# A two-layer windowed transformer on one NeuronCore: the second tile's values, queries and transposes moved, and the exponential's table loaded earlier

## The chip, the cores and the metric

The kernel runs on one core of one Trainium2 chip. The core has five engines, each with its own instruction queue, worked off in order: PE (TensorE, matrix products and transposes), ACT (ScalarE, functions and copies), DVE (VectorE), POOL (GpSimd) and SP (SyncE, which only issues transfers here). PE writes to PSUM, 128 partitions by eight banks of 512 float32 columns; ACT and DVE read PSUM, POOL doesn't. The metric is the time of one execution in microseconds (us).

## The reference

Eight batches of 256 tokens with 256 channels. First a gated cross-attention, then two layers of a local-attention transformer with a gated GELU, all in float32:

```python
x = x + tanh(g_xattn) * xattn(layernorm(x), ctx, ctx, mask)       # one head of 256
y = layernorm(x)
for l in range(2):
    h = shift_token(y)                       # half of the channels come from the token before
    q, k, v = split(h @ wqkv[l], 3)          # 8 heads of 64
    q, k = rotary(l2norm(q) * q_scale, l2norm(k) * k_scale)
    o = local_attention(q, k, v)             # window of 128: a token sees its own and the previous window
    y = y + o @ wo[l]
    h = layernorm(shift_token(y)) * ln_g + ln_b
    a, g = split(h @ w1[l] + b1[l], 2)       # 682 hidden channels
    y = y + (a * gelu(g)) @ w2[l] + b2[l]
x = x + tanh(g_ffn) * y
```

## The kernel before

A first stage does the cross-attention of the eight batches. Then come 17 steps. Step s does the attention half of one batch in one layer (batch s, layer 0 for s below 8, then layer 1) together with the feed-forward half of the batch of step s-1; step 0 has only an attention half, step 16 only a feed-forward half. Steps 2 to 7 and 9 to 14 are two loops on the engines ("loop steps" below); 0, 1, 8, 15 and 16 are written out. Every engine's order within a step is written by hand; semaphores join the engines. The 256 tokens are two tiles, t = 0 and 1, of 128 rows. Float32 products are made of three products of rounded high and low parts (`split_product`, L422).

On PE a step runs: `project` (queries, keys and values of both tiles, j = 0, 1, 2; tile 0 uses banks 0, 1, 2, tile 1 banks 3, 4 and, for its values, bank 2 again), then `up(0)` to `up(5)`, the first feed-forward product in six chunks in banks 5 and 6 by turns, with the transposes of queries and keys (`tr_heads(t, j)`, L580) in between. Then `scores_own(0)` (L592) and `scores_both(0)` (L598) for the first two heads, five pieces `down(0)` to `down(4)` of the second feed-forward product, and a loop over heads h of `scores`, `tr_probs(h)` (transposes of the probabilities, L607 to L609), more `down`, and `weighted` (L621). Last come the transposes of the next batch and the output projection.

The other engines, per head h: DVE's `row_min(h)` (L1153) masks the scores and takes each row's minimum, ACT's `exps(h)` (L855) takes the exponentials, DVE's `row_sum(h)` (L1159) the reciprocals of their sums, POOL's `normalise(h)` (L1357) multiplies, PE transposes, ACT's `probs_T(h)` (L861) copies.

In the feed-forward half, for each chunk c: ACT's `gelu(c)` (L825, the sixth L828), DVE's `gated(c)` (L1134), ACT's `high_u(c)` (L834, chunks 0 to 4), POOL's `low_u(c)` (L1339), PE's `down(c)`. The last chunk has 42 rows, and its high part is cast by DVE (`high_last_u`, L1142), which waits until ACT has done `high_u(4)`. PE's `down(4)` waits for `low_u(4)`, which needs `high_u(4)` too. Before `low_u(4)` POOL does an addition (L1381).

ACT also copies values (`values(t)`, L818), transposed queries (`queries_T(t)`, L840) and keys (`keys_T(t)`, L846) out of PSUM. Its function tables hold one set at a time; a Gelu after an Exp, and the other way round, needs an `ACT_TABLE_LOAD`. The Gelu's is brought forward by a dummy activation of one column, `table_touch` (L895); the Exp's stands right ahead of `exps(0)`.

Of the kernel before, what the change touches and what calls it, by code (L numbers as in the profile page):

```python
# [18 lines left out]
P = 128  # L19
# [4 lines left out]
ACT = mybir.ActivationFunctionType  # L24
# [5 lines left out]
HEADS, DH = 8, 64  # L30
# [19 lines left out]
def build(nc, x, ctx_in, mask, g_xattn, g_ffn, Wq, bq, Wk, bk, Wv, bv, ln_gamma, ln_beta,  # L50
          wqkv, q_scale, k_scale, wo, ln_g, ln_b, w1, b1, w2, b2, rot_tab, win_mask, ident_in, shift_in, out):
    NB, S, D = x.shape
    T = S // P
# [22 lines left out]
    with st:  # L76
# [3 lines left out]
        def sem(name):  # L80
            return st.enter_context(nc.semaphore(name))
# [83 lines left out]
        def bank(i):  # L165
            return ps[:, i, :]
# [7 lines left out]
        w_high, w_ready, w2_ready = sem("w_high"), sem("w_ready"), sem("w2_ready")  # L174
        b1_mm, b1_done, w1_scaled = sem("b1_mm"), sem("b1_done"), sem("w1_scaled")
        zeros_set, nhalf_set, tanh_done, prep_done = sem("zeros_set"), sem("nhalf_set"), sem("tanh_done"), sem("prep_done")
        touch_set = sem("touch_set")
        dve_passed, pool_passed = sem("dve_passed"), sem("pool_passed")

        x_loaded, c_loaded, m_loaded, xres_loaded = (  # L180
# [227 lines left out]
        def _(pe):  # L408
# [113 lines left out]
            def step(s, la, lf):  # L522
                f = s - 1

                def project(t, parts):

                    i = 0 if t == 0 else 3
                    if t == 0 and 0 in parts:
                        pe.wait_ge(yT_done, s + 1)
                        if isinstance(s, int) and s == 0:  # L530
                            pe.wait_ge(xnT_done, NB)
                            pe.wait_ge(kT_x, KC * NB)
                            pe.wait_ge(qT_x, KC * NB)
                            pe.wait_ge(v_x, NB)
                    elif 0 in parts:
                        wait(pe, pT_done, HEADS * s)
                    for j in parts:
                        if j == 2:
                            if t == 0:
                                wait(pe, x1_done, s)  # L540
                            else:
                                pe.wait_ge(v_done, T * s + t)
                        if t == 0 and isinstance(s, int) and s in (0, NB):
                            pe.wait_ge(w_ready, VPIECES * la + j + 1)
                        o = bank(i + j) if j < 2 else bank(2)
                        for k in range(KC):
                            c0 = k * YTC - k + t * P
                            last = split_product(o, lambda a: yT[a][:, c0:c0 + P],
                                                 lambda a: wqkv_hl[a][:, k, j * INNER:(j + 1) * INNER],
                                                 k == 0, k == KC - 1)  # L550
                        last.then_inc((qk_mm, qk_mm, v_mm2)[j], 1)

                def up(c):

                    i = 5 + c % 2
                    if c == 0:
                        pe.wait_ge(hT_done, s)
                        if lf == 1 or (isinstance(s, int) and s == 1):
                            pe.wait_ge(w_ready, VPIECES * (lf + 1))
                            pe.wait_ge(w2_ready, 2 * (lf + 1))  # L560
                    if c < 2:
                        pe.wait_ge(o_done, PAIRS * s)
                    else:
                        pe.wait_ge(u_raw, HC * f + c - 1)
                    for o, r, n in up_parts(c):
                        for k in range(KC):
                            last = split_product(ps[0:r, i, n * S:(n + 1) * S],
                                                 lambda a: w1_hl[a][:, k, o:o + r], lambda a: hT[a][:, k, :],
                                                 k == 0, k == KC - 1)
                    last.then_inc(up_mm, 1)  # L570

                def tr_heads(t, j):

                    i = 0 if t == 0 else 3
                    if j == 0:
                        pe.wait_ge(sq_done, 2 * (T * s + t + 1))
                    if j == 0:
                        pe.wait_ge(ks_done, T * s + t + 1)
                    for c in range(PAIRS):
                        last = nc.tensor.transpose(bank(i + j)[:, c * P:(c + 1) * P],  # L580
                                                   t1[:, t, j * INNER + c * P:j * INNER + (c + 1) * P],
                                                   ident[:])
                    last.then_inc(qk_tr, 1)
# [44 lines left out]
                def down(n):  # L628

                    t, c = n // HC, n % HC  # L630
                    if t == 0:
                        pe.wait_ge(u_done, HC * f + c + 1)
                    last = split_product(bank(7)[:, t * D:(t + 1) * D], lambda a: u[a][:, c, t * P:(t + 1) * P],
                                         lambda a: w2_hl[a][:, c, :], c == 0, c == HC - 1)
                    if n == T * HC - 1:
                        last.then_inc(dn_mm, 1)
# [39 lines left out]
                if A:  # L676
                    tr_heads(0, 1)
                if F:
                    for c in range(3, HC):
                        up(c)  # L680
                if A:
                    tr_heads(1, 0)
                    tr_heads(1, 1)
                if A:
                    pe.wait_ge(q_done, T * s + 1)
                    pe.wait_ge(k_done, T * s + 1)
                    pe.wait_ge(v_done, T * (s + 1))
                    scores_own(0)
                    pe.wait_ge(q_done, T * (s + 1))
                    pe.wait_ge(k_done, T * (s + 1))  # L690
                    scores_both(0)
                n = 0
                if A and F:
                    for n in range(HC - 1):
                        down(n)
                    n = HC - 1
                if A:
                    for h in range(HEADS + 1):
                        if h in (0, 1, 3):
                            scores_own((h + 3) // 2)  # L700
                            scores_both((h + 3) // 2)
                        if h < HEADS:
                            tr_probs(h)
                        if isinstance(s, int) and s in (0, NB) and h == HEADS - 1:
                            bias_products(la)
                        if F:
                            while (n - HC + 1) * HEADS < (T * HC - 2 - HC + 1) * h:
                                down(n)
                                n += 1
                        if h and h % 2 == 0:  # L710
                            weighted(h // 2 - 1)
                    if not (isinstance(s, int) and s == STEPS - 1):
                        pe.wait_ge(ynext_in, 16 * (s + 2))
                        pe.wait_ge(mn_done, T * HEADS * (s + 1))
                        transpose_rows(y_next, 0).then_inc(y_tr, 1)
# [20 lines left out]
        def _(act):  # L736
# [68 lines left out]
            def step(s, la, lf):  # L805
# [9 lines left out]
                def values(t):  # L815
                    act.wait_ge(v_mm2, T * s + t + 1)
                    wait(act, pv_mm, HEADS * s)
                    A(vs[:, t, :], bank(2), ACT.Copy).then_inc(v_done, 1)  # L818

                def gelu(c):  # L820
                    act.wait_ge(up_mm, HC * f + c + 1)
# [9 lines left out]
                def high_u(c):  # L831
                    act.wait_ge(u_raw, HC * f + c + 1)
                    r = hrows[c]
                    A(u[0][0:r, c, :], u_full[c % 4][0:r, :], ACT.Copy).then_inc(u_high, 1)  # L834

                def queries_T(t):
                    i = 0 if t == 0 else 3
                    act.wait_ge(qk_tr, 2 * (T * s + t) + 1)
                    wait(act, s_mm2, HEADS * s)
                    A(qT[:, :, t * P:(t + 1) * P], bank(i).rearrange("p (c n) -> p c n", c=PAIRS),  # L840
                      ACT.Copy).then_inc(q_done, 1)

                def keys_T(t):
                    i = 0 if t == 0 else 3
# [55 lines left out]
                    gelu(1)  # L900
                    high_u(0)
                if la is not None:
                    queries_T(0)
                if lf is not None:
                    gelu(2)
                if la is not None:
# [1 line left out]
                if lf is not None:  # L908
                    high_u(1)
                    gelu(3)  # L910
                    high_u(2)
                    gelu(4)
                    high_u(3)
                    gelu(5)
                if la is not None:
                    queries_T(1)
                    keys_T(1)
                if lf is not None:
                    high_u(4)
                if la is not None:  # L920
# [18 lines left out]
        def _(dve):  # L939
# [131 lines left out]
            def step(s, la, lf):  # L1071
# [95 lines left out]
                def row_statistics():  # L1167
# [6 lines left out]
                    for t in range(T):  # L1174
                        wait_apart(dve, dve_passed, (hbn_a, 2 * (T * f + t + 1)))
                        V.bn_aggr(hmv[:, t, :], hst[:, t, :, :]).then_inc(hbn, 1)  # L1176

                start = isinstance(s, int) and s == 0
                if isinstance(s, int) and s == NB:
                    low_parts(1, True)  # L1180
# [35 lines left out]
                    add_context(NB - 1)  # L1216
                if F:
                    gated(4)
                    gated(5)
                    high_last_u()  # L1220
                if start:
# [223 lines left out]
```

## Time and profile before

| what | value |
|---|---|
| median of three runs | 821.9 us (819.35 to 823.16) |
| the profiled execution's own time | 824.24 us |
| its span, first to last instruction | 822.4 us |
| busy: PE, DVE, ACT, POOL | 730.5, 527.0, 486.9, 437.2 us |
| mean granted clock of PE | 0.964 |

The span leaves 1.8 us of the profiled execution's time outside it. Busy time says how long an engine had an instruction under way, not what held the others up; that is read from the waits and from the chain of work that ended last. A loop step takes 40.8 us (its first square on ACT starts at 327.36 in step 5 and at 368.15 in step 6).

### The profile page before, as it was taken

Reading aid. Unit: us, or ns where it says so; the run is one execution under the profiler, and the core shown is the slowest. Engines: PE = TensorE matmul, PEld = TensorE weight load, DVE = VectorE, ACT = ScalarE, POOL = GpSimd, SP = SyncE. Lnnn points to the kernel's source line nnn. Section 1 sums busy time; section 2 is a strip of 40 time slices with the busy share of each in tenths; the row PEclk is TensorE's granted clock in tenths of the full one; section 3 lists DMA queues with packets and bytes.
Section 4 is the critical chain, followed back from the end, with each engine's and each line's share of the span. In section 5 each row is a group of like instructions: output and inputs, shape, how many; then the busy total and the mean of one; then the engine's idle time right before and its main releaser. Section 6 shows DMA issues by size and latency. Waiting matters only on the chain.

```text
span 822.4 us, 17078 instructions
## 1 busy us (share of the span) xinstructions
PE 730.5 (89%) x4984; PEld 608.3 (74%) x4984; DVE 527.0 (64%) x1470; ACT 486.9 (59%) x1289; POOL 437.2 (53%) x592
## 2 busy tenths in 40 slices
PE   5898766989999999999998998999999999999967
PEld 4787654877878787878786877877777777777746
DVE  2898896384848484847475836657575766666732
ACT  2443425366767575757577665757575757575742
POOL 0433464473838383838383646738383737373712
PEclk9999987799999999999999998999999999999988
DMA  6444423160000000000101001010101010101000
GB/s 209 144 149 140 125 47 108 48 232 16 24 17 23 21 18 24 14 32 6 37 2 38 1 2 51 2 52 0 51 0 51 0 51 0 51 0 39 1 27 13
DMA packets 32786, 38.36 MB, mean 47 GB/s; under 512 B 8476, under 2 KB 22896, under 8 KB 32752
## 3 DMA queue, kind: packets, MB, share of 16 engines
q1 hardware_dynamic: 32752, 37.95, 14.4%
q8 instruction: 16, 0.26, 0.1%
q14 instruction: 18, 0.15, 0.1%
HBM read 29.55 MB, written 8.39 MB: 46 GB/s over the span
## 4 chain that ended last, share of the span: by engine, by line
PE 56%; DVE 13%; ACT 11%; issue 10%; POOL 5%; DMA 3%; SPq 1%; DVEq 1%; ACTq 0%; POOLq 0%
PE ps L422 39%; ACT pr L855 4%; PE ps L621 4%; PE ps L598 3%; DMA arena<-x 2%; PE ps L517 2%; DVE arena L955 2%; PE ps L580 2%; PE ps L592 1%; PE ps L415 1%; POOL xrs L1275 1%; ACT pT L861 1%; PE ps L625 1%; DVE sm L1153 1%; POOL pr L1357 1%
## 5 line engine op out<-in xcount | busy, mean ns | idle before, releaser
L1357 POOL TENSOR_SCALAR pr<-pr,rl 128x128 f32<-128x128 f32 (+1 forms) x256 | 107.6, 433 | 80.5 <-DVE rl L1159 80.4
L855 ACT ACTIVATE pr<-sm,mn 128x128 f32<-128x128 f32 (+1 forms) x256 | 113.4, 445 | 20.6 <-DVE mn L1153 20.1
L1153 DVE CUSTOM_DVE_ANT_0 sm<-ps,wmask 128x128 f32<-128x128 f32 (+1 forms) x256 | 79.9, 354 | 44.4 <-PE ps L598 38.5
L422 PE MATMUL ps<-hT_hi,w_hi 128*128 128x256 f32 (+1 forms) x352 | 103.4, 294 | 1.7 <-DVE hT_lo L1125 1.4
L422 PE MATMUL ps<-hT_hi,w_lo 128*128 128x256 f32 (+1 forms) x352 | 101.0, 287 | 0.0
L422 PE MATMUL ps<-hT_lo,w_hi 128*128 128x256 f32 (+1 forms) x352 | 100.2, 285 | 0.0
L1328 POOL TENSOR_TENSOR rn<-ss,nhalf 128x16 f32<-128x16 f32 x32 | 96.7, 3023 | 2.7
L813 ACT ACTIVATE sqb<-ps 128x512 f32<-128x512 f32 x64 | 38.0, 596 | 95.5 <-PE ps L422 88.6
L422 PE MATMUL ps<-wqkv_hi,yT_hi 128*128 128x512 f32 x192 | 80.3, 418 | 12.5 <-DVE arena L997 5.2
L1273 POOL TENSOR_SCALAR hrs<-hmv 128x2 f32<-128x2 f32 x16 | 3.1, 193 | 150.6 <-DVE hmv L1176 150.6
L1339 POOL TENSOR_TENSOR u_lo<-u_pair,u_hi 128x256 fp32r<-128x256 f32 x64 | 68.9, 1085 | 23.8 <-ACT u_hi L834 21.7
L422 PE MATMUL ps<-wqkv_lo,yT_hi 128*128 128x512 f32 x192 | 77.1, 402 | 0.0
L422 PE MATMUL ps<-wqkv_hi,yT_lo 128*128 128x512 f32 x192 | 77.0, 401 | 0.0
L825 ACT ACTIVATE gl<-ps,b_sb 128x256 f32<-128x256 f32 x80 | 38.0, 475 | 58.6 <-PE ps L422 58.6
L422 PEld LDWEIGHTS ps<-hT_hi,w_hi 128*128 128x128 f32 (+1 forms) x352 | 67.6, 192 | 4.7 <-DVE hT_lo L1125 2.5
L422 PEld LDWEIGHTS ps<-hT_lo,w_hi 128*128 128x128 f32 (+1 forms) x352 | 67.9, 193 | 0.1
L422 PEld LDWEIGHTS ps<-hT_hi,w_lo 128*128 128x128 f32 (+1 forms) x352 | 67.2, 191 | 0.0
L861 ACT ACTIVATE pT<-ps 128x384 f32<-128x384 f32 x128 | 61.2, 480 | 7.9 <-PE ps L609 6.9
L422 PE MATMUL ps<-w_hi,u_hi 128*128 128x256 f32 x192 | 64.0, 333 | 1.4 <-POOL u_lo L1339 1.3
L607 PE MATMUL ps<-ident,pr 128*128 128x128 f32 x128 | 41.6, 325 | 20.1 <-POOL pr L1357 17.9
L1146 DVE TENSOR_TENSOR oT_lo<-ps,oT_hi 128x256 fp32r<-128x256 f32 x64 | 27.1, 423 | 49.7 <-ACT oT_hi L866 48.1
L607 PEld LDWEIGHTS ps<-ident,pr 128*128 128x128 f32 x128 | 17.9, 140 | 51.8 <-POOL pr L1357 48.9
(148 smaller groups left out, 2129.8 us busy)
## 6 DMA issues: line engine op xcount, KB each, us to landing
arena<-x SPq DMA_DIRECT2D x16, 256.0 KB, 3.5
ystream<-arena SPq DMA_DIRECT2D x16, 256.0 KB, 2.0
y_next<-ystream SPq DMA_DIRECT2D x16, 256.0 KB, 2.8
y_res<-ystream SPq DMA_DIRECT2D x16, 256.0 KB, 2.6
arena<-L_ffn_w SPq DMA_DIRECT2D x6, 640.0 KB
arena<-ctx SPq DMA_DIRECT2D x8, 256.0 KB, 3.9
arena<-mask_BxSxS_ik SPq DMA_DIRECT2D x8, 256.0 KB, 2.8
xmid<-arena SPq DMA_DIRECT2D x8, 256.0 KB, 2.0
```

The costliest lines, as they stand in the source:

```text
L422: last = mm(out, lhsT(a), rhs(b), start=(start and i == 0), stop=(stop and i == 2))
L607: nc.tensor.transpose(b[:, 0:P], p[:, 2 * P:3 * P], ident[:])
L621: mm(b[j * DH:(j + 1) * DH, 0:S], vs[:, 0, h * DH:(h + 1) * DH], pT[:, h % 4, P:3 * P], start=True, stop=False)
L813: A(sqb[:, j * INNER:(j + 1) * INNER], bank(i + j), ACT.Square).then_inc(sq_done, 1)
L825: A(gl[:, c % 2, :], ps[:, 5 + c % 2, S:2 * S], ACT.Gelu, bias=b1_sb[:, lf, 1, c:c + 1]).then_inc(gl_done, 1)
L855: A(pr[:, h % NS, a:b], sm[:, h % NS, a:b], ACT.Exp, bias=mn[:, h, t:t + 1], scale=-1.0, accum_out=ls[:, h, t:t + 1]).then_inc(e_done, 1)
L861: A(pT[:, h % 4, :], bank(3 + h % 2)[:, 0:3 * P], ACT.Copy).then_inc(pT_done, 1)
L1146: V.tensor_tensor(oT[1][:, pair, :], bank(5 + pair % 2)[:, 0:S], oT[0][:, pair, :].bitcast(F32), ALU.subtract).then_inc(o_done, 1)
L1153: V.tensor_tensor_reduce(sm[:, h % NS, a:b], bank(h % SB)[:, a:b], wmask[:, a:b], 1.0, -NEG, ALU.add, ALU.min, mn[:, h, t:t + 1]).then_inc ...
L1328: G.tensor_tensor(rn[:, t, :], ss[:, t, :], nhalf[:], ALU.pow).then_inc(rn_done, 1)
L1339: G.tensor_tensor(u[1][0:r, c, :], u_full[c % 4][0:r, :], u[0][0:r, c, :].bitcast(F32), ALU.subtract).then_inc(u_done, 1)
L1357: G.tensor_scalar(pr[:, h % NS, a:b], pr[:, h % NS, a:b], rl[:, h, t:t + 1], 1.0, ALU.mult, ALU.mult).then_inc(pn_done, 1)
```

## The change

Four things move within a step. Tile 1's values go to bank 6 instead of bank 2, so their product no longer waits for ACT to empty bank 2; it waits for bank 6's last user in the step before, and `up(1)`, which writes bank 6 next, waits for both copies of values. Tile 1's transposed queries are copied by DVE, between `gated(4)` and `gated(5)`, with a semaphore of their own (`q1_done`), instead of by ACT. Tile 1's transposes stand ahead of `up(5)` instead of behind it, and ACT's `keys_T(1)` ahead of `high_u(3)`. And ACT does a dummy exponential of one column right behind `gelu(5)`, ahead of `high_u(4)`. The order of the `down` pieces is written another way and stays what it was.

```diff
@@ PE: project
                             else:
-                                pe.wait_ge(v_done, T * s + t)
+                                wait(pe, o_done, PAIRS * s)
...
-                        o = bank(i + j) if j < 2 else bank(2)
+                        o = bank(i + j) if j < 2 else bank(2 + 4 * t)
@@ PE: up(c)
                     if c < 2:
                         pe.wait_ge(o_done, PAIRS * s)
+                        if c == 1 and la is not None:
+                            pe.wait_ge(v_done, T * (s + 1))
@@ PE: step
                 if F:
-                    for c in range(3, HC):
+                    for c in range(3, HC - 1):
                         up(c)
                 if A:
                     tr_heads(1, 0)
                     tr_heads(1, 1)
+                if F:
+                    up(HC - 1)
...
                     scores_own(0)
-                    pe.wait_ge(q_done, T * (s + 1))
+                    pe.wait_ge(q1_done, s + 1)
                     pe.wait_ge(k_done, T * (s + 1))
                     scores_both(0)
@@ ACT: values(t)
-                    A(vs[:, t, :], bank(2), ACT.Copy).then_inc(v_done, 1)
+                    A(vs[:, t, :], bank(2 + 4 * t), ACT.Copy).then_inc(v_done, 1)
@@ ACT: step
                     gelu(4)
+                if la is not None:
+                    keys_T(1)
+                if lf is not None:
                     high_u(3)
                     gelu(5)
                 if la is not None:
-                    queries_T(1)
-                    keys_T(1)
+                    A(table_touch[:, 1:2], table_touch[:, 0:1], ACT.Exp)
                 if lf is not None:
                     high_u(4)
@@ DVE
+                def queries_T():
+                    dve.wait_ge(qk_tr, 2 * (T * s + 1) + 1)
+                    wait(dve, s_mm2, HEADS * s)
+                    V.tensor_copy(qT[:, :, P:S], bank(3).rearrange("p (c n) -> p c n", c=PAIRS)).then_inc(q1_done, 1)
...
                 if start:
                     context(NB - 1)
                     gate_context(NB - 1)
                     add_context(NB - 1)
                 if F:
                     gated(4)
+                if A:
+                    queries_T()
+                if F:
                     gated(5)
                     high_last_u()
```

ACT's queue in a loop step, from `gelu(4)` to the first exponential, before (`gl` is a gelu's result, `u_hi` a high part, `qT` and `kT` the copied queries and keys, `pr` the exponentials):

```order
L825 ACTIVATE gl<-ps,b_sb 128x256 [waits u_raw,up_mm]
L834 ACTIVATE u_hi<-hn 128x256 [waits u_raw]
L821 REGISTER_ALU
L828 ACTIVATE gl<-ps,b_sb 42x256 [waits u_raw,up_mm]
L840 ACTIVATE qT<-ps 128x4x128 [waits s_mm2,qk_tr]
L846 ACTIVATE kT<-ps 128x4x128 [waits qk_tr]
L834 ACTIVATE u_hi<-u_pair 128x256 [waits u_raw]
L850 ISA
L855 ACT_TABLE_LOAD [waits rl_done]
L855 ACTIVATE pr,ls<-sm,mn 128x128 [waits mn_done]
```

and the same stretch of the changed kernel:

```order
L830 ACTIVATE gl<-ps,b_sb 128x256 [waits u_raw,up_mm]
L849 ACTIVATE kT<-ps 128x4x128 [waits qk_tr]
L839 ACTIVATE u_hi<-hn 128x256 [waits u_raw]
L826 REGISTER_ALU
L833 ACTIVATE gl<-ps,b_sb 42x256 [waits u_raw,up_mm]
L922 ACT_TABLE_LOAD
L922 ACTIVATE table_touch<-table_touch 128x1
L839 ACTIVATE u_hi<-u_pair 128x256 [waits u_raw]
L853 ISA
L858 ACTIVATE pr,ls<-sm,mn 128x128 [waits rl_done,mn_done]
```

The keys moved up, the queries are gone, and the table load with its dummy now stands ahead of the fifth high part instead of behind it.

DVE's queue in the written-out step 0 of the changed kernel, from the last additions of the first stage (`arena`, `xst`, `xmv`) to the first `row_min` (`sm`, `mn`):

```order
L987 TENSOR_TENSOR arena<-arena 128x512 [waits xmid_stored,xrb_done,tg_done]
L952 BN_STATS xst<-arena 128x6 [waits xmid_done]
L952 BN_STATS xst<-arena 128x6
L955 BN_AGGR xmv<-xst 128x2 [waits stats_mid] x2
L1186 COPY qT<-ps 128x4x128 [waits qk_tr]
L1158 ISA sm,mn<-ps,wmask 128x128 [waits cst2_in,s_mm2]
L1158 ISA mn 128x1
L1158 ISA sm,mn<-ps,wmask 128x256
```

Here the copy of queries stands behind what is left of the first stage, right ahead of the first `row_min`; before, the rows around it were the same without it, and ACT made that copy.

## Rows read from the trace of the kernel before

**Rows 1.** Chain of work that ended last, step 5: start us, us, what

```profile
345.73 0.60 ACT kT L846
...
347.17 1.98 PE ps L422 x15
```

**Rows 2.** Timeline of PE, step 5: start us, us, instruction, idle before

```profile
334.26 0.50 PE L422 MATMUL ps<-wqkv_hi,yT_hi 128*128 128x512 f32 x1 [0.33 <-ACT vs L818]
...
335.76 0.28 PE L422 MATMUL ps<-hT_hi,w_hi 128*128 128x256 f32 x1
...
343.74 0.28 PE L422 MATMUL ps<-hT_hi,w_hi 128*106 128x256 f32 x1
...
344.45 1.04 PE L580 MATMUL ps<-ident,turned 128*128 128x128 f32 x8
...
346.47 0.70 PE L598 MATMUL ps<-kT,qT 64*128 64x256 f32 x4 [0.56 <-ACT kT L846]
...
350.57 0.33 PE L607 MATMUL ps<-ident,pr 128*128 128x128 f32 x1 [0.56 <-POOL pr L1357]
...
352.04 0.33 PE L607 MATMUL ps<-ident,pr 128*128 128x128 f32 x1
...
353.18 0.33 PE L607 MATMUL ps<-ident,pr 128*128 128x128 f32 x1 [0.24 <-POOL pr L1357]
```

**Rows 3.** Timeline of ACT, step 5

```profile
336.01 0.20 ACT L895 ACTIVATE table_touch<-table_touch 128x1 f32<-128x1 f32 x1
...
344.74 0.47 ACT L828 ACTIVATE gl<-ps,b_sb 42x256 f32<-42x256 f32 x1
...
346.35 0.42 ACT L834 ACTIVATE u_hi<-u_pair 128x256 fp32r<-128x256 f32 x1
346.78 1.28 ACT L855 ACT_TABLE_LOAD   x1
348.11 0.40 ACT L855 ACTIVATE pr<-sm,mn 128x128 f32<-128x128 f32 x1
```

**Rows 4.** Timeline of DVE, step 5

```profile
334.82 0.68 DVE L1125 TENSOR_TENSOR hT_lo<-ps,hT_hi 128x512 fp32r<-128x512 f32 x1
...
346.80 0.29 DVE L1142 CAST u_hi<-u_pair 42x256 fp32r<-42x256 f32 x1 [1.08 <-ACT u_hi L834]
347.43 0.29 DVE L1153 CUSTOM_DVE_ANT_0 sm<-ps,wmask 128x128 f32<-128x128 f32 x1 [0.34 <-PE ps L598]
```

**Rows 5.** Timeline of POOL, step 5

```profile
345.48 1.26 POOL L1381 TENSOR_TENSOR arena<-x,b_bc 128x512 f32<-128x512 f32 x1
346.84 1.52 POOL L1339 TENSOR_TENSOR u_lo<-u_pair,u_hi 128x256 fp32r<-128x256 f32 x2
...
351.15 0.84 POOL L1357 TENSOR_SCALAR pr<-pr,rl 128x128 f32<-128x128 f32 x2 [0.63 <-DVE rl L1159]
```

**Rows 6.** Timeline of POOL and DVE in step 1, which is written out

```profile
183.78 0.73 POOL L1339 TENSOR_TENSOR u_lo<-u_pair,u_hi 128x256 fp32r<-128x256 f32 x1 [0.51 <-ACT u_hi L834]
183.81 0.85 DVE L1142 CAST u_hi<-u_pair 42x256 fp32r<-42x256 f32 x1 [1.14 <-ACT u_hi L834]
184.58 0.28 DVE L1153 CUSTOM_DVE_ANT_0 sm<-ps,wmask 128x128 f32<-128x128 f32 x1
```

**Rows 7.** Timeline of DVE and PE in step 0

```profile
131.83 0.29 DVE L1153 CUSTOM_DVE_ANT_0 sm<-ps,wmask 128x128 f32<-128x128 f32 x1
...
133.12 1.06 PE L598 MATMUL ps<-kT,qT 64*128 64x256 f32 x4
...
134.36 0.29 DVE L1153 CUSTOM_DVE_ANT_0 sm<-ps,wmask 128x128 f32<-128x128 f32 x1 [0.67 <-PE ps L598]
```

**Rows 8.** Chain of work that ended last, end of step 0

```profile
140.48 5.80 DMA arena<-L_ffn_w
146.33 7.45 PE ps L517 x44
```

**Rows 9.** Two stretches: length; busy PE, PEld, DVE, ACT, POOL; PE's clock; DMA

```profile
508.00:512.00 4.00, 2.18 (x10) 1.43 (x8) 3.92 (x8) 2.16 (x6) 2.94 (x6) 1.00 0.00 0
512.00:516.00 4.00, 3.63 (x14) 2.90 (x15) 3.55 (x6) 3.54 (x7) 3.92 (x3) 0.72 0.02 4
```

More of the change, by code:

```diff
@@ L176, in build @@
         zeros_set, nhalf_set, tanh_done, prep_done = sem("zeros_set"), sem("nhalf_set"), sem("tanh_done"), sem("prep_done")
-        touch_set = sem("touch_set")
+        touch_set, q1_done = sem("touch_set"), sem("q1_done")
         dve_passed, pool_passed = sem("dve_passed"), sem("pool_passed")
@@ L683, in step, with downs @@
                     tr_heads(1, 1)
+                if F:
+                    up(HC - 1)
+                n = 0
+                def downs(upto):
+                    nonlocal n
+                    while F and n < upto:
+                        down(n)
+                        n += 1
                 if A:
-                    pe.wait_ge(q_done, T * s + 1)
+                    pe.wait_ge(q_done, s + 1)
                     pe.wait_ge(k_done, T * s + 1)
@@ L688, in step @@
                     scores_own(0)
-                    pe.wait_ge(q_done, T * (s + 1))
+                    pe.wait_ge(q1_done, s + 1)
                     pe.wait_ge(k_done, T * (s + 1))
                     scores_both(0)
[L692 to L697, printed above, removed]
+                    downs(5)
                     for h in range(HEADS + 1):
@@ L705, in step @@
                             bias_products(la)
[L706 to L709, printed above, removed]
+                        downs(5 + min(5, (5 * h + 7) // 8))
                         if h and h % 2 == 0:
@@ L834, in high_u @@
                     A(u[0][0:r, c, :], u_full[c % 4][0:r, :], ACT.Copy).then_inc(u_high, 1)
-                def queries_T(t):
-                    i = 0 if t == 0 else 3
-                    act.wait_ge(qk_tr, 2 * (T * s + t) + 1)
+                def queries_T():
+                    act.wait_ge(qk_tr, 2 * T * s + 1)
                     wait(act, s_mm2, HEADS * s)
-                    A(qT[:, :, t * P:(t + 1) * P], bank(i).rearrange("p (c n) -> p c n", c=PAIRS),
-                      ACT.Copy).then_inc(q_done, 1)
+                    A(qT[:, :, 0:P], bank(0).rearrange("p (c n) -> p c n", c=PAIRS), ACT.Copy).then_inc(q_done, 1)
                 def keys_T(t):
@@ L902, in step @@
                 if la is not None:
-                    queries_T(0)
+                    queries_T()
                 if lf is not None:
@@ L1176, in row_statistics, with queries_T @@
                         V.bn_aggr(hmv[:, t, :], hst[:, t, :, :]).then_inc(hbn, 1)
+                def queries_T():
+                    dve.wait_ge(qk_tr, 2 * (T * s + 1) + 1)
+                    wait(dve, s_mm2, HEADS * s)
+                    V.tensor_copy(qT[:, :, P:S], bank(3).rearrange("p (c n) -> p c n", c=PAIRS)).then_inc(q1_done, 1)
                 start = isinstance(s, int) and s == 0
@@ L1218, in step @@
                     gated(4)
+                if A:
+                    queries_T()
+                if F:
                     gated(5)
```

## The prediction

> **What bounds the kernel now.** I read the chain of work that ended last first, then the timelines of PE, ACT, DVE and POOL over one loop step, step 5, and then the written-out steps 0 and 1. The other eleven loop steps repeat step 5 to a few hundredths of a microsecond. In the chain the reader is to see that PE carries most of a step, and that it is handed to other engines where PE waits: ACT's copy of keys, then scores and five `down` pieces [rows 1]. PE's own timeline shows four waits in step 5 that the change touches: 0.33 us for ACT's copy of values, 0.56 for ACT's copy of keys ahead of `scores_both(0)`, 0.56 for POOL ahead of `tr_probs(0)`, 0.24 ahead of `tr_probs(2)` [rows 2]. From `tr_probs(2)` on the chain runs without slack to the step's end. So what counts is when `tr_probs(2)` starts.
>
> **Values in a bank of their own.** `project(1, 2)` no longer waits, but `up(0)`, right behind it, needs DVE's low part, which ends at 334.82 + 0.68 = 335.50 [rows 4]. PE follows a release by about 0.14 (keys end at 346.33, `scores_both(0)` starts at 346.47 [rows 1, 2]), so `up(0)` starts at 335.64 instead of 335.76: 0.12 gained, not 0.33. The new wait of `up(1)` for both values costs nothing: ACT copies the second right behind its `table_touch` at 336.01 [rows 3], 0.6 us long like the keys, and `up(1)` comes twelve products behind `up(0)`.
>
> **Transposes ahead of `up(5)`.** They start where `up(5)` did, at 343.74 - 0.12 = 343.62, and end 1.04 later, 344.66; `up(5)` is pushed back by about 0.87 (the record of 1.04 less a drain that overlaps, my estimate) and its result is there at about 345.4 [rows 2].
>
> **ACT.** `keys_T(1)` 344.69 to 345.29 (0.60 [rows 1]), `high_u(3)` to 345.6, `gelu(5)` 345.62 to 346.09, which is 0.88 later than now. Then the table load, 1.28, the touch, 0.20 of which the next instruction overlaps some 0.1, and only then `high_u(4)`: 347.51 to 347.92 instead of 346.35 to 346.77, 1.15 later [rows 3]. The load itself is no new cost, since one stands in each step now; at present it lies beside `row_min(0)`, and ends at 348.06, just when `exps(0)` can start at 348.11. The cover that it loses is that: `high_u(4)` used to be ahead of it, and three engines wait for `high_u(4)`.
>
> **Who waits for it.** DVE's cast of the last chunk waits for it by semaphore, and `row_min(0)` is queued behind the cast: cast 347.95, `row_min(0)` at about 348.27 instead of 347.43, and `exps(0)`, 0.68 behind it as now, at 348.95 instead of 348.11, 0.84 later [rows 3, 4]. POOL's addition is done by then (its `low_u(3)` moves with `high_u(3)`, so it ends at about 347.6), and `low_u(4)` runs 347.99 to 348.72, 1.15 later than now [rows 5]. PE's `scores_both(0)` has its queries from DVE (344.8 to 345.4, priced as the 0.68 of DVE's other 512-column instruction from PSUM [rows 4]) and starts at 345.6 instead of 346.47. That gain of 0.87 is given back at once: four `down` pieces of 0.4 each later PE stands at `down(4)`, about 347.8, until `low_u(4)` at 348.76; the five pieces end at 349.25, against 347.17 + 1.98 = 349.15 now [rows 1]. So `scores(1)` is 0.1 later, and everything that hangs on `exps(0)` is 0.84 later: its reciprocal, POOL's multiplication and `tr_probs(0)`, which goes from 350.57 to 351.41 [rows 2].
>
> **What slack takes up.** Behind `tr_probs(0)` PE's queue holds scores, `tr_probs(1)`, a `down`, `tr_probs(2)`. The last waited 0.24, and `tr_probs(1)` at 352.04 came 0.05 behind POOL's 351.15 + 0.84 [rows 2, 5], so some slack lies there as well. I put both at 0.35 and have 0.5 us left per loop step (between 0.3, if the slack is 0.5, and 0.7). Twelve loop steps: 6.0 us.
>
> **Written-out steps 1, 8, 15.** There the cast already takes 0.85 and `row_min(0)` starts right behind it, without waiting for PE [rows 6]. So all of `high_u(4)`'s 1.15 reaches `exps(0)`, less 0.35: 0.8 each, 2.4 us (0.5 to 1.1 each; step 1 may be the low end, since DVE holds its `up(5)` back).
>
> **Step 0.** No feed-forward half, no cast, and the table is already Exp's. But the copy of queries, which ACT did early, now stands on DVE behind the rest of the first stage, where `row_min(0)` started at 131.83. Copy 0.68, answer of PE 0.14, and from the start of such a pair of scores to its `row_min` 134.36 - 133.12 = 1.24 [rows 7]: 2.06 later, 2.0 in the sum. The step's chain runs on over a store, the feed-forward weights' load and the products that wait for them at 146.33 [rows 8], and that load is issued behind DVE work which follows `row_min(2)`; nothing hides it. Bounds: 0.7, the copy alone, if PE's part were hidden, to 2.1. Step 16 is unchanged.
>
> **Sum.** 6.0 + 2.4 + 2.0 = 10.4 us on the profiled execution's 824.24, so 834.6. That execution lies 2.3 over the median of 821.9; for a median I say 832. With the bounds (12 x 0.3 to 0.7, 3 x 0.5 to 1.1, 0.7 to 2.1) 5.8 to 13.8, hence 828 to 836 for this case.
>
> **Rivals.**
> - *The cast is blocked in the loop steps too.* In step 1 POOL's `low_u(4)` started 0.03 ahead of the cast, and the cast took 0.85, until POOL's 0.73 had passed; in step 5 the cast came first by 0.04 and took 0.29 [rows 4 to 6]. In step 5 POOL was then busy with its addition until 346.74; in the changed kernel it will be waiting for `high_u(4)` as in step 1. Then `row_min(0)` comes 0.77 behind the cast's start, not 0.32: 0.45 to 0.55 more in twelve steps, 6 us, 838. Against it: in the loop steps DVE woke 0.03 after ACT's end, POOL takes 0.07. I go by the short cast. The Trainium skill (SBUF — State Buffer, "Who interferes with whom") calls the port pair that DVE's copies and POOL share an exclusive lock that goes to whoever issues first; by that rule it hangs on those 0.04 us, and the sum would be the one or the other.
> - *The delay is taken up.* If PE's slack behind `tr_probs(0)` is as large as 0.84, only the 0.1 of `scores(1)` counts in a loop step: 1.2 + 1 + 2.0, about 826. For it: `exps(2)` hangs on `scores(1)`, not on `exps(0)`. Against it: PE shows only 0.24 of wait there.
> - *Faster.* If `high_u(4)` came no later than now, the wait of 0.56 ahead of `scores_both(0)` and the 0.12 would be won in 15 steps, 10 us, with step 0's loss 814. It decides at `high_u(4)` ending by 346.8 in step 5's time. Against it stands the load's 1.28 in ACT's queue, ahead of it, and `gelu(5)` behind the transposes.
> - *PE's clock falls.* PE would stand 1.0 us at `down(4)` and 1.2 at `tr_probs(0)`. Around step 9's start PE was busy 2.18 of 4 us, and the granted clock then averaged 0.72 over 4 us, part of it at the lower of the two levels, 1.2 GHz [rows 9]. Some 1.2 us per step, 12 steps: 846. Against it: that stall was one piece.
> - *It does nothing:* the order shows every piece moved, so I give this none of its own.
>
> **How the numbers follow.** Forecast 0.62, blocked cast 0.13, taken up 0.13, faster 0.05, clock 0.07. About 0.5%, 4.1 us, is what a measurement of this kernel can tell from no change: faster below 817.8, slower above 826.0. Faster is the third rival, 0.05; same is the second, 0.13, and 0.01 of others; the rest, 0.81, is slower. The range from 825 to 840 takes in the forecast, the blocked cast and half of the second rival, 0.8 in all.
>
> **What would show it.** In the changed trace: `scores_both(0)` without a wait for keys, 0.8 us earlier behind `up(4)`; a wait of about 1 us ahead of `down(4)` on POOL's `low_u(4)`; the table load right behind `gelu(5)`; DVE's wait ahead of the cast grown from 1.08 to over 1.5 and the cast's length (0.29 or 0.85); `tr_probs(0)`'s wait on POOL over 1 us; the loop step's length, 41.3 against 40.8; in step 0 `row_min(0)` about 2 us later. A `high_u(4)` less than 0.5 us late, or PE not waiting ahead of `tr_probs(0)`, would make the prediction wrong.

## The result, and the profile after

The changed kernel takes 832.41 us (median), the kernel before 821.69 on the same chip: 1.0141 times as long, 95% interval 1.0108 to 1.0175. Forecast were 832 us and a range of 825 to 840. The profiled execution took 832.07 us; its span is 830.3 us, 7.9 more than before, and PE is as busy as before (730.6 us).

Step 5 starts 0.93 us later than before (its first square stands at 328.29 instead of 327.36). Whoever takes 0.93 off the rows below can lay them beside [rows 2 to 5]. A step now lasts 41.17 us, before 40.79. First PE's timeline, step 5 of the changed kernel:

```profile
334.61 0.48 PE L422 MATMUL ps<-wqkv_hi,yT_hi 128*128 128x512 f32 x1
...
336.49 0.38 PE L422 MATMUL ps<-hT_hi,w_hi 128*128 128x256 f32 x1 [0.23 <-DVE hT_lo L1130]
...
344.57 1.03 PE L582 MATMUL ps<-ident,turned 128*128 128x128 f32 x8
...
346.57 0.60 PE L600 MATMUL ps<-kT,qT 64*128 64x256 f32 x4
...
349.82 0.38 PE L422 MATMUL ps<-w_hi,u_hi 128*128 128x256 f32 x1 [1.03 <-POOL u_lo L1352]
...
350.16 0.28 PE L422 MATMUL ps<-w_hi,u_lo 128*128 128x256 f32 x1
350.37 0.49 PE L594 MATMUL ps<-kT,qT 64*128 64x128 f32 x4
...
352.38 0.33 PE L609 MATMUL ps<-ident,pr 128*128 128x128 f32 x1 [1.08 <-POOL pr L1370]
...
354.47 0.33 PE L609 MATMUL ps<-ident,pr 128*128 128x128 f32 x1
```

The waits for values (0.33) and keys (0.56) are gone. In their place PE stands 1.03 us at `down(4)` for POOL's `low_u(4)` (349.82), and 1.08 instead of 0.56 at `tr_probs(0)` (352.38). The 0.24 ahead of `tr_probs(2)` (354.47) is gone too: there slack was used up. Next ACT's timeline in the same step:

```profile
346.57 0.47 ACT L833 ACTIVATE gl<-ps,b_sb 42x256 f32<-42x256 f32 x1
347.06 1.28 ACT L922 ACT_TABLE_LOAD   x1
348.35 0.20 ACT L922 ACTIVATE table_touch<-table_touch 128x1 f32<-128x1 f32 x1
348.46 0.40 ACT L839 ACTIVATE u_hi<-u_pair 128x256 fp32r<-128x256 f32 x1
349.92 0.40 ACT L858 ACTIVATE pr<-sm,mn 128x128 f32<-128x128 f32 x1 [1.06 <-DVE mn L1158]
```

The load lies between `gelu(5)` and `high_u(4)`, and ACT then waits 1.06 us for DVE's minimum: the early load left nothing for ACT to do. DVE's timeline shows why the minimum is late, with the queries' copy first, then the cast behind `high_u(4)`, then `row_min(0)`:

```profile
345.68 0.68 DVE L1186 COPY qT<-ps 128x512 f32<-128x512 f32 x1
...
348.89 0.28 DVE L1147 CAST u_hi<-u_pair 42x256 fp32r<-42x256 f32 x1 [1.34 <-ACT u_hi L839]
349.25 0.29 DVE L1158 CUSTOM_DVE_ANT_0 sm<-ps,wmask 128x128 f32<-128x128 f32 x1
```

On POOL's timeline `low_u(4)` waits for the same `high_u(4)`; the addition ahead of it had ended 0.35 us before. `low_u(4)` starts 0.05 behind DVE's cast and takes 0.83 us, where it took 0.73 in step 1 [rows 6]:

```profile
347.30 1.28 POOL L1394 TENSOR_TENSOR arena<-x,b_bc 128x512 f32<-128x512 f32 x1
348.94 0.83 POOL L1352 TENSOR_TENSOR u_lo<-u_pair,u_hi 128x256 fp32r<-128x256 f32 x1 [0.35 <-ACT u_hi L839]
```

In step 1, which is written out, POOL is ahead of the cast by 0.03, as in [rows 6], and the cast is long again (POOL's and DVE's timelines):

```profile
183.96 0.72 POOL L1352 TENSOR_TENSOR u_lo<-u_pair,u_hi 128x256 fp32r<-128x256 f32 x1 [0.35 <-ACT u_hi L839]
...
183.99 0.85 DVE L1147 CAST u_hi<-u_pair 42x256 fp32r<-42x256 f32 x1 [1.42 <-ACT u_hi L839]
```

In step 0 the copy of queries stands where `row_min(0)` stood (DVE's timeline):

```profile
131.15 0.66 DVE L1186 COPY qT<-ps 128x512 f32<-128x512 f32 x1
133.25 0.29 DVE L1158 CUSTOM_DVE_ANT_0 sm<-ps,wmask 128x128 f32<-128x128 f32 x1 [1.45 <-issue]
```

The first stage ended 0.57 us earlier in this execution (its last statistics start at 130.81, before at 131.38), so without the copy `row_min(0)` would have stood at 131.26 instead of 131.83 [rows 7]. It is 1.99 later. From there the delay does not run by the load of [rows 8] here: the products that read the weights start without a wait, right behind PE's transposes of the last probabilities (PE's timeline):

```profile
147.69 0.27 PE L611 MATMUL ps<-ident,pr 128*128 128x128 f32 x1
147.80 5.14 PE L517 MATMUL ps<-lgb,arena 128*128 128x1 f32 x44
```

Last, three stretches of step 10 of the changed kernel, PE alone: bounds, then length, PE's busy time, its granted clock as a share of 2.4 GHz, DMA's share and rate.

```profile
572.00:574.00 2.00, 0.96 (x9) 1.00 0.00 0
574.00:576.00 2.00, 1.00 (x10) 0.92 0.00 0
576.00:578.00 2.00, 2.00 (x11) 0.50 0.00 0
```

There, around the two new waits, PE was busy for 1.96 of 4 us, and the clock then went to 1.2 GHz (0.50) until about 579. Step 10 lasts 42.55 us, 1.31 more than step 11 (41.24). The same happened at this place in step 8 (480 to 487) and step 15 (784 to 787), not in the eleven other loop steps with much the same waits. In the profile of before no step has a low stretch at this place. Another profile of nearly the same kernel (step 0's queries by ACT, below) shows the falls of steps 8 and 15 again, and none at this place in a loop step.

### The profile page after: what moved, and what is told of

Same layout as the page of the kernel before. It is cut to its first block, busy times and chain, and to the rows that moved or that the text cites. A ratio compares the mean times of both kernels' runs of the same rounds, so it can differ in the third digit from the quotient of the medians.

```text
span 830.3 us, 17109 instructions
## 1 busy us (share of the span) xinstructions
PE 730.6 (88%) x4984; PEld 607.8 (73%) x4984; DVE 535.6 (65%) x1486; ACT 482.2 (58%) x1289; POOL 436.6 (53%) x592
## 4 chain that ended last, share of the span: by engine, by line
PE 46%; ACT 11%; DVE 11%; issue 10%; POOL 5%; DVEq 1%; ACTq 0%; POOLq 0%
PE ps L422 26%; PE ps L623 4%; ACT pr L858 4%; PE ps L582 3%; ACT L922 2%; PE ps L609 2%; PE ps L600 2%; PE ps L594 2%; DVE ss L1082 2%; DVE turned L1096 2%; POOL rn L1341 1%; PE ps L627 1%; ACT pT L864 1%; POOL pr L1370 1%; PE ps L415 1%
## 5 line engine op out<-in xcount | busy, mean ns | idle before, releaser
L422 PE MATMUL ps<-hT_hi,w_hi 128*128 128x256 f32 (+1 forms) x352 | 105.3, 299 | 5.4 <-DVE hT_lo L1130 5.4
L1352 POOL TENSOR_TENSOR u_lo<-u_pair,u_hi 128x256 fp32r<-128x256 f32 x64 | 70.9, 1116 | 23.4 <-ACT u_hi L839 22.7
L422 PE MATMUL ps<-w_hi,u_hi 128*128 128x256 f32 x192 | 66.3, 345 | 16.6 <-POOL u_lo L1352 16.5
L1151 DVE TENSOR_TENSOR oT_lo<-ps,oT_hi 128x256 fp32r<-128x256 f32 x64 | 27.1, 423 | 49.7 <-ACT oT_hi L869 48.1
L609 PEld LDWEIGHTS ps<-ident,pr 128*128 128x128 f32 x128 | 18.2, 142 | 52.8 <-POOL pr L1370 44.8
```

What stands on the lines that cost most here:

```text
L422: last = mm(out, lhsT(a), rhs(b), start=(start and i == 0), stop=(stop and i == 2))
L609: nc.tensor.transpose(b[:, 0:P], p[:, 2 * P:3 * P], ident[:])
L1151: V.tensor_tensor(oT[1][:, pair, :], bank(5 + pair % 2)[:, 0:S], oT[0][:, pair, :].bitcast(F32), ALU.subtract).then_inc(o_done, 1)
L1352: G.tensor_tensor(u[1][0:r, c, :], u_full[c % 4][0:r, :], u[0][0:r, c, :].bitcast(F32), ALU.subtract).then_inc(u_done, 1)
```

## Experiments

All ratios are against the kernel before, timed alongside; its median was 820.75, 821.76 and 821.40 us in the three groups of experiments, so the times of two rows can be 1 us further apart or closer than the kernels are. "Loop step" is the length of one step, taken as half of what steps 12 and 13 last together, against before's 40.87 us there; in these two no profile shows a low clock.

| kernel | us | ratio (95%) | loop step |
|---|---|---|---|
| changed | 832.4 | 1.0141 (1.0108 to 1.0175) | +0.36 |
| touch alone | 831.6 | 1.0140 (1.0113 to 1.0167) | +0.58 |
| bank alone | 819.8 | 0.9965 (0.9948 to 0.9983) | -0.10 |
| changed, no touch | 823.1 | 1.0029 (1.0010 to 1.0048) | -0.09 |
| changed, touch behind `high_u(4)` | 822.6 | 1.0018 (1.0005 to 1.0032) | -0.08 |
| changed, step 0's queries by ACT | 832.2 | 1.0143 (1.0119 to 1.0167) | +0.36 |
| no touch, step 0's queries by ACT | 822.7 | 0.9996 (0.9971 to 1.0022) | -0.06 |
| changed, cast behind | 828.5 | 1.0082 (1.0059 to 1.0105) | +0.37 |
| changed, `down(4)` behind | 842.9 | 1.0256 (1.0218 to 1.0295) | +0.51 |
| changed, both behind | 825.1 | 1.0035 (1.0016 to 1.0055) | -0.36 |
| no touch, cast behind | 820.3 | 0.9978 (0.9958 to 0.9997) | -0.12 |
| no touch, addition early | 813.2 | 0.9885 (0.9852 to 0.9919) | -0.72 |
| all together | 806.0 | 0.9798 (0.9767 to 0.9829) | -0.93 |

**Without the dummy exponential, and with it one place later.** In ACT's step:

```diff
                     gelu(5)
-                if la is not None:
-                    A(table_touch[:, 1:2], table_touch[:, 0:1], ACT.Exp)
                 if lf is not None:
                     high_u(4)
```

> The changed kernel without its dummy exponential, so that the table load stands right ahead of exps(0) again. Theory T1 (the load ahead of high_u(4) is what costs): high_u(4) then comes right behind gelu(5), 0.2 us earlier than in the kernel before, PE no longer stands at down(4), and exps(0) follows the load, which ends about 1.3 + 0.4 us behind gelu(5), 0.25 us earlier than before the change. With scores(1) 0.8 us earlier I expect 0.25 to 0.5 us less than before in each of 15 steps, so a time of 814 to 818 us, step 0 still late by 2. Rival T2 (the transposes ahead of up(5) and the queries in DVE's queue cost, not the load): 828 us or more. Rival T3 (PE's clock falls at the new waits and that is most of the loss): between 822 and 828, with the low stretches gone from the steps and little else.

In the second kernel these two lines stand behind `high_u(4)`.

> The changed kernel with the dummy exponential moved one place, behind high_u(4) instead of ahead of it. T1: as without the dummy, 814 to 818 us, since the load then stands at the same place; the dummy's 0.1 us more per step at most, 1.5 in all. T2: 828 or more. A third possibility is that the explicit dummy starts the load earlier than the automatic one, which is issued with exps(0): then up to 0.3 us per step better than without the dummy.

Measured: 823.07 and 822.61. So the touch's place ahead of `high_u(4)` costs nine of the eleven microseconds, and T2 falls. T3's range holds both times, but not its account: the loop step is 0.45 us shorter than in the changed kernel, which is 5.4 of the 9.3 us in twelve steps, without the clock. T1 has the cause, and misses the time: the expected gain over the kernel before is not there. The step without the touch is shorter than before by what the bank alone gives. Its profile says why (timelines of DVE, POOL and ACT, step 5, 0.39 earlier than before):

```profile
346.37 1.06 DVE L1145 CAST u_hi<-u_pair 42x256 fp32r<-42x256 f32 x1
347.35 0.27 DVE L1156 CUSTOM_DVE_ANT_0 sm<-ps,wmask 128x128 f32<-128x128 f32 x1
...
346.00 1.29 POOL L1392 TENSOR_TENSOR arena<-x,b_bc 128x512 f32<-128x512 f32 x1
347.24 1.47 POOL L1350 TENSOR_TENSOR u_lo<-u_pair,u_hi 128x256 fp32r<-128x256 f32 x2
...
346.19 1.28 ACT L858 ACT_TABLE_LOAD   x1
348.01 0.40 ACT L858 ACTIVATE pr<-sm,mn 128x128 f32<-128x128 f32 x1 [0.54 <-DVE mn L1156]
```

`high_u(4)` now comes 0.21 earlier than before the change, while POOL is still in its addition. The cast starts 0.37 behind the addition's start and lasts until 0.14 behind its end, 1.06 instead of 0.28 us; `low_u(4)` can't start before that either. So `row_min(0)`, `exps(0)` and `down(4)` came later than I had worked out, by a neighbour that the late `high_u(4)` had kept out of sight. The Trainium skill (SBUF — State Buffer, "Who interferes with whom") has casts among the DVE operations that can take the port pair shared with GpSimd, and calls that pair an exclusive lock, held for the whole instruction by whoever issues first. By that rule the cast waits out the whole addition; the trace agrees (1.06).

**The touch alone.** The two touch lines ahead of `high_u(4)` in the kernel before, nothing else.

> The kernel before with nothing but the dummy exponential, ahead of high_u(4). T1: high_u(4) 1.4 us later, row_min(0) and exps(0) 1.1 later, of which 0.5 is slack behind tr_probs(0): 0.5 to 0.6 us in each of 15 steps, so 829 to 831 us, about as slow as the whole change. T2: no change, 822. If the clock falls at the new waits in some steps, up to 4 us more.

831.57: the one line makes the kernel before as slow as the whole change, with 0.58 a step, as T1 had it. (The profile has one fall of the clock in a loop step; step 4 is 1.5 us longer than step 5.) ACT's timeline, step 5 (1.63 later than before):

```profile
347.98 1.28 ACT L919 ACT_TABLE_LOAD   x1
349.38 0.40 ACT L834 ACTIVATE u_hi<-u_pair 128x256 fp32r<-128x256 f32 x1
350.86 0.40 ACT L855 ACTIVATE pr<-sm,mn 128x128 f32<-128x128 f32 x1 [1.07 <-DVE mn L1155]
```

**Values in bank 6 alone.** Of the change's diff, the lines of `project`, `up(c)` and `values(t)`, in the kernel before.

> The kernel before with nothing but the second tile's values in bank 6. My term: project(1, 2) no longer waits 0.33 us, but up(0) behind it waits for DVE's low part, so 0.12 us per step are left, 15 steps, 1.8 us: 820 us. Rival A: all of the 0.33 is won, 817. Rival B: the wait of up(1) for both copies of values takes it back: 822.

819.76, 0.10 a step: my term. `up(0)` waits for DVE's low part, as said (PE's timeline, step 5):

```profile
336.22 0.38 PE L422 MATMUL ps<-hT_hi,w_hi 128*128 128x256 f32 x1 [0.23 <-DVE hT_lo L1127]
```

**The two ways from `high_u(4)` to the step's end.** In the changed kernel, `high_last_u()` moved on DVE in every step with both halves:

```diff
                     gated(5)
+                if F and not A:
                     high_last_u()
...
                     row_min(0)
                     row_min(1)
+                if A and F:
+                    high_last_u()
```

> The changed kernel with DVE's cast of the last chunk moved behind row_min(0) and row_min(1). Path P1 (high_u(4), cast, row_min(0), exps(0), tr_probs(0)): row_min(0) no longer waits for high_u(4), exps(0) follows high_u(4) directly, 1.0 us earlier, tr_probs(0) 0.9 earlier; if this path alone makes a loop step 0.38 longer than before the change, that is gone: 12 x 0.38, about 827 us. Path P2 (high_u(4), low_u(4), down(4), scores(1), exps(2), tr_probs(2)), which in the profile is late by 0.36 us, the same amount: if it binds as well, the step stays as long as it is, 832.

and, apart from it, `down(4)` on PE:

```diff
-                    downs(5)
+                    downs(4)
                     for h in range(HEADS + 1):
```

> The changed kernel with down(4) moved behind tr_probs(0), so that scores(1) doesn't stand behind low_u(4). P1 alone binds: tr_probs(0) stays 0.88 us late, and down(4), 0.4 us of PE, comes into the slack behind it: no gain, or up to 0.4 us per loop step more, 832 to 838. P2 alone binds: scores(1) comes 1.3 us earlier, 827. Both bind: 832 or a little more.

and both:

> Both moves at once in the changed kernel: the cast behind row_min(0) and row_min(1), down(4) behind tr_probs(0). The load still stands ahead of high_u(4). If the late high_u(4) costs by these two paths and no other, the loop steps become as short as before the change or up to 0.3 us shorter, since PE's wait for keys is gone: 818 to 826 us. If there is a third path: 830 or more.

With the cast behind, the time fell to 828.47, but the loop step kept its +0.37. PE's timeline, step 5 (4.18 later than before):

```profile
353.06 0.39 PE L422 MATMUL ps<-w_hi,u_hi 128*128 128x256 f32 x1 [1.04 <-POOL u_lo L1356]
...
354.68 0.33 PE L609 MATMUL ps<-ident,pr 128*128 128x128 f32 x1
...
357.72 0.33 PE L609 MATMUL ps<-ident,pr 128*128 128x128 f32 x1 [0.24 <-POOL pr L1374]
```

`tr_probs(0)` is back where it was (354.68 - 4.18 = 350.50), without a wait, yet `tr_probs(2)` is at 353.54, exactly as in the changed kernel (354.47 - 0.93). So P2 binds as well, by the same 0.36. What was won, some 4 us, is not in the loop steps' length; this profile has none of the low stretches in steps 8, 10 and 15. With `down(4)` behind, P1 binds and `down(4)` comes on top of it; PE then waits twice, longer (its timeline, step 5):

```profile
353.23 0.49 PE L594 MATMUL ps<-kT,qT 64*128 64x128 f32 x4 [1.16 <-DVE mn L1158]
...
355.68 0.33 PE L609 MATMUL ps<-ident,pr 128*128 128x128 f32 x1 [1.51 <-POOL pr L1370]
```

It lost more (842.85) than I had allowed for; its profile has low stretches behind these waits in steps 2, 6, 8, 9, 10, 11 and 14. With both behind, the loop step is 0.36 shorter than before the change: there is no third path. The time, 825.1, is above the kernel before all the same. In its step PE stands once:

```profile
353.40 0.33 PE L609 MATMUL ps<-ident,pr 128*128 128x128 f32 x1 [1.79 <-POOL pr L1374]
```

and its clock fell in four loop steps (271, 393, 574 and 738 us), each 1.5 us longer than its neighbours. Twelve times -0.36, four falls of 1.5 and step 0's 2.3 (below) make +4.0; the medians differ by 3.3. That is a sum over one profile, not a test, but by it the falls behind the one long wait gave back what the shorter step had won.

**Step 0.** Its queries copied by ACT, in the changed kernel and in the one without the touch:

```diff
+                if isinstance(s, int) and s == 0:
+                    act.wait_ge(qk_tr, 2 * (T * s + 1) + 1)
+                    A(qT[:, :, P:S], bank(3).rearrange("p (c n) -> p c n", c=PAIRS), ACT.Copy).then_inc(q1_done, 1)
...
-                if A:
+                if A and not start:
                     queries_T()
```

> The changed kernel with the copy of the second tile's queries made by ACT in step 0 alone, as before the change. My theory of step 0: its first row_min comes 2.0 us earlier against the first stage, and the feed-forward weights' load with it, so 2.0 us less in all, 830.4 us. Rival: PE's clock, which in the changed kernel's profile stood at its low level for a shorter part of the weights' products (from 152.7 instead of 148.8 us), falls earlier again, and takes the 2.0 back: 832.4, with row_min early all the same.

> The changed kernel without the dummy exponential, and in step 0 the queries copied by ACT; a second try at step 0's price, beside the same kernel with DVE's copy (823.07, twelve runs). My term: 2.0 us, 821. Rival: the clock in the first stage and in the weights' products takes it back, 823.

The medians (832.22 beside 832.41; 822.67 beside 823.07) don't show 2 us; their intervals, 2 to 3 us to each side, can't tell it from nothing. The profiles can. The first `row_min` starts 2.44 us behind the start of the first stage's last statistics in each of the eight profiles with DVE's copy, 0.45 behind it in each of the six with ACT's: 1.99. From the first square of step 0 to the first of step 1 it takes 52.2 to 55.0 us (mean 53.3) with DVE's copy, 49.6 to 52.4 (mean 51.0) with ACT's: 2.3 us. The spread within each kind goes with PE's clock: it is low for 3.4 to 10.3 us of the work that begins with the weights' products, and for 13.6 to 23.9 us of what comes before. Where both are alike (20.5, then 6.8 us low) it takes 52.4 to 52.8 in three profiles with DVE's copy and 49.6 or 49.7 in two with ACT's. In these two stretches of the kernel before, and of the changed one below it, the columns are length; PE, PEld, DVE, ACT and POOL busy; clock; DMA:

```profile
148.00:152.00 4.00, 4.00 (x23) 4.00 (x22) 0.00 (x0) 0.00 (x0) 0.00 (x0) 0.56 0.00 0
152.00:156.00 4.00, 4.00 (x21) 3.18 (x21) 0.64 (x4) 0.38 (x1) 2.02 (x2) 0.50 0.01 4
```

```profile
148.00:152.00 4.00, 4.00 (x38) 4.00 (x38) 0.40 (x1) 0.49 (x1) 0.00 (x0) 1.00 0.02 7
152.00:156.00 4.00, 4.00 (x23) 2.95 (x23) 0.81 (x4) 0.89 (x3) 2.83 (x2) 0.55 0.02 4
```

The 44 products of the weights began 1.47 later than before (147.80 instead of 146.33 [rows 8]), but took 5.14 instead of 7.45 us: in this pair of profiles the clock gave back what the copy had cost, as the rival had it.

**Taking the addition out of the way.** In POOL's step, on the changed kernel without the touch:

```diff
-                        if c == HC - 2:
+                        if c == HC - 3:
                             pool.wait_ge(x1_done, s)
```

> The changed kernel without the dummy exponential, and with POOL's addition one place earlier, ahead of low_u(3) instead of low_u(4). In the profile without the dummy the addition ran from 346.28 to 347.57 (in the time of the kernel before), and both the cast (346.65, 1.06 us long) and low_u(4) (347.52) ended or began behind it. Theory T4 (the addition took the gain): low_u(4) starts 1.0 us earlier, PE no longer stands at down(4) and scores(1) comes 0.6 earlier; the cast is still up to 0.85 long, beside low_u(4) now, so row_min(0) and exps(0) come 0.25 earlier at most. 0.25 to 0.4 us per step less than without this move, 817 to 820 us beside 823. Rival T5 (the step is bound by PE from tr_probs(0) on, whatever comes earlier): 823.

(By the first square of step 5 that profile lies 0.39 us ahead of the kernel before, so the addition ran from 346.39 to 347.68 in before's time; the argument stays.)

With the cast behind `row_min(1)` instead, and with everything together:

> The changed kernel without the dummy exponential, and with DVE's cast behind row_min(0) and row_min(1); the addition stays. T4: row_min(0) no longer stands behind a cast that waits out the addition, and exps(0) follows the table load, 0.5 us earlier; but low_u(4), low_u(5) and with them POOL's first multiplication and scores(1) stay where they are: 0 to 0.2 us per step, 820 to 823 us. If the cast alone was the brake: 0.5 us per step, 816.

> All together: the changed kernel without the dummy exponential, the cast behind row_min(0) and row_min(1), POOL's addition ahead of low_u(3), and in step 0 the queries copied by ACT. T4: exps(0) at the end of the table load, 0.3 us earlier than before the change, scores(1) 0.8 earlier, tr_probs(0) 0.6 earlier, so 0.4 to 0.6 us per step less than in the kernel before, and nothing lost in step 0: 810 to 816 us. T5: 820. If PE's clock falls at some of the waits that are left, 1.2 to 1.5 us for each fall.

813.18, 820.34 and 806.0. T4 has the cause and mis-sizes it: the addition's move gives 0.63 a step, not 0.25 to 0.4, and both kernels with it are faster than their ranges; T5 falls. One place for POOL's addition is worth 10 us once the touch is gone (12 by the ratios). The cast's alone gives 2.7 by the medians, of which the loop steps show 0.3 (twelve times 0.03). PE's timelines say why the two differ so, step 5 with the cast moved (0.51 earlier than before) and, below it, with the addition moved (0.05 earlier):

```profile
347.89 0.39 PE L422 MATMUL ps<-w_hi,u_hi 128*128 128x256 f32 x1 [0.54 <-POOL u_lo L1354]
```

```profile
348.11 0.49 PE L594 MATMUL ps<-kT,qT 64*128 64x128 f32 x4
...
350.52 0.33 PE L609 MATMUL ps<-ident,pr 128*128 128x128 f32 x1 [1.48 <-POOL pr L1368]
...
352.60 0.27 PE L609 MATMUL ps<-ident,pr 128*128 128x128 f32 x1
```

With the cast alone moved, PE still waits at `down(4)` for `low_u(4)`, which stands behind the addition. With the addition moved, `tr_probs(0)` stands where it stood before the change (350.57), but `scores(1)` comes 0.92 earlier (348.16 for 349.08) and `tr_probs(2)` 0.53 earlier (352.65 for 353.18): the gain comes by path P2.

With everything together the kernel takes 0.98 times as long as before. Step 5 there (4.23 earlier than before), timelines of POOL, DVE, ACT and PE:

```profile
342.39 0.74 POOL L1357 TENSOR_TENSOR u_lo<-u_pair,u_hi 128x256 fp32r<-128x256 f32 x1 [0.21 <-ACT u_hi L839]
...
342.30 0.27 DVE L1159 CUSTOM_DVE_ANT_0 sm<-ps,wmask 128x128 f32<-128x128 f32 x1
...
343.41 0.28 DVE L1148 CAST u_hi<-u_pair 42x256 fp32r<-42x256 f32 x1
...
341.89 0.42 ACT L839 ACTIVATE u_hi<-u_pair 128x256 fp32r<-128x256 f32 x1
342.33 1.28 ACT L858 ACT_TABLE_LOAD   x1
343.62 0.40 ACT L858 ACTIVATE pr<-sm,mn 128x128 f32<-128x128 f32 x1
...
346.09 0.33 PE L609 MATMUL ps<-ident,pr 128*128 128x128 f32 x1 [1.26 <-POOL pr L1375]
```

The load stands behind `high_u(4)` and beside `row_min(0)`, whose minima are ready when it ends: `exps(0)` starts 0.01 behind the load. That is the cover which the change had taken away.

## Why the prediction was right, and where its sum was not

The mechanism was right in nearly every step. That the total came to 0.4 us was luck: inside the sum two terms were too large and one, PE's clock, was left out, and these made up for each other.

- **Bank, transposes, `gelu(5)`.** 0.10 a step for 0.12; `gelu(5)` 0.90 later (345.64 in before's time) for 0.88. Right.
- **The load ahead of `high_u(4)`.** 1.18 later for 1.15; cast short (0.28), `row_min(0)` at 348.32 for 348.27, `exps(0)` at 348.99 for 348.95, `tr_probs(0)` 0.88 later for 0.84. Right, and shown to be the cause by the touch alone and by its removal. DVE's wait ahead of the cast was 1.34, not over 1.5: I had not counted that `gated(5)`, behind the late `gelu(5)`, shortens it.
- **"scores(1) is 0.1 later".** Mis-sized: 0.36 (349.44 for 349.08). `low_u(4)` started as forecast, but took 0.83 beside the cast where I had put 0.73, and `down(4)`, begun anew behind a wait, took 0.62 (349.82 to 350.44) where I had put 0.49; with 0.03 at the two starts that is the 0.26 above the 0.1. So a second path bound as hard as the first, as the cast moved behind showed.
- **"some slack lies there: 0.35".** Mis-sized: `tr_probs(0)` 0.88 later became `tr_probs(2)` 0.36 later, so 0.52 was taken up. A loop step cost 0.36 to 0.38 for 0.5; twelve steps 4.4 us for 6.0.
- **Written-out steps, 0.8 each.** Too large for step 1: `high_u(4)` was only 0.43 later there against the step's own start, and slack took it all (the step lasts 42.88 us for 43.07). Of the 0.75 that lack, 0.27 is a wait of PE for DVE ahead of `up(5)`, which the transposes filled; the rest was there early in the step, at ACT's third square (4.14 us behind the first for 4.69), and why stays open. In step 15 the cast was 1.27 later than in the step's own time before, as the term had it.
- **Step 0, 2.0.** 1.99 at `row_min(0)`, 2.3 in the step's length over the fourteen profiles. Right in size; the path behind it was not the load alone, since in the changed kernel's profile PE's own transposes, later by the same copy, held the products up.
- **PE's clock.** I gave it 0.07 and thought of a fall in every step. It fell in three of fifteen, at 1.31 us where a neighbour shows the price. About 4 us of the 10.7 are left beside 4.4 and 2.3; the kernel with the cast behind, same loop step and no such falls, is about 4 us faster. Part of that may be the delay by P1 in steps 8 and 15 (the sum's 0.8 each), which went with it; no run separates the two. Why the clock fell in step 10 and not in the eleven steps like it stays open.

The rival of a blocked cast did not come in the loop steps of the changed kernel, where DVE was again ahead, by 0.05; it came in the kernel without the touch, by another instruction of POOL.

## What to carry to other kernels

A table load cost nothing here where its engine would have waited anyway; before moving one, ask which instruction behind it has readers on other engines, and put it behind that one. When an experiment removes a delay and the time stays, look for a neighbour that the delay had hidden: here an addition on POOL, worth about as much as the whole change had cost. And look at a step's longest wait as well as at its length: in the profiles here PE's clock fell behind such waits, in four of twelve loop steps with one of 1.79 us, in one of twelve with 1.03 and 1.08, in none of the kernel before with 0.56.

## What the runs showed of the hardware that I had not expected

- A cast on DVE of 0.28 us took 0.77 behind POOL's 0.74 (no touch, addition early), 0.85 behind 0.72 (step 1) and 1.06 behind the rest of 1.29 (no touch): it ends 0.14 to 0.16 behind POOL's end each time. The same cast took 0.28 when it began 0.05 ahead of POOL, and POOL's instruction then 0.83 instead of 0.73.
- PE's clock takes different courses in nearly the same work: in the first stage and the weights' products of step 0 its low stretches add up to 27 to 38 us in the fourteen profiles, and the length of step 0 differs by 2.8 us within each of the two kinds, more than its term of the prediction.
